# One block for layer norm and feed-forward in a six-layer decoder kernel

## The chip, the core and the metric

The kernel runs on one core of one Trainium2 chip. Its engines each follow an instruction stream of their own: TensorE (PE in the profile, PEld for its weight loads), VectorE (DVE), ScalarE (ACT), GpSimd (POOL) and SyncE (SP, here only a queue that issues DMAs). They meet through semaphores. The metric is the device time of one execution in microseconds (us), lower is better; the number compared is the median of several executions.

## The reference

The program computes a decoder of two layers on x (4 sequences of 256 tokens, 256 columns, so 1024 tokens in 8 tiles of 128). Each layer is self-attention, cross-attention and a feed-forward part, each on a layer norm of x and added to x. The change concerns the feed-forward part of the first layer:

```python
def activation_quant(x, num_bits=8):
    s = qp / jnp.clip(jnp.max(jnp.abs(xf), axis=-1, keepdims=True), EPS, None)   # qp = 127, qn = -128
    return (jnp.clip(jnp.round(xf * s), qn, qp) / s).astype(x.dtype)
...
h = jax.nn.silu(bit_linear(x, w_gate)) * bit_linear(x, w_up)    # 256 -> 1024 columns
h = rms_norm(h, ln_weight)
return bit_linear(h, w_down)                                     # 1024 -> 256
...
x = x + _L0_ffn_ref(_layernorm(x, axis=-1), ...)
```

bit_linear multiplies the quantised activations by weights rounded to -1, 0, 1 times a mean. The second cross-attention, two stages later, uses the input ctx_512 (1024 tokens, 64 columns) as keys and values of 8 groups.

## The kernel before

The program is a sequence of blocks. Inside a block every engine has its own stream; at a block's end all engines and the issued DMAs that the block waits for must be done before the next block starts. The order within a stream is written out by hand. `TT` is 8 token tiles, `c.x` the residual stream, `c.ps` the 8 PSUM banks, `wb` the ternary weights in bf16.

The feed-forward part (`ffn_stages`) is three blocks. First `layer_norm` writes normalised tiles to `c.xn` (L200 to L217). Then comes the gate/up block: VectorE takes the largest magnitude of all eight tiles in one reduction (L1871), makes the factors, and quantises all tiles by multiply and min, max and add of the rounding constant, subtract (L1885 to L1893); TensorE turns all 16 quarter tiles (L1909), ScalarE copies them out (L1940), and then for each tile TensorE makes gate and up products in four PSUM banks (L1919), ScalarE applies silu to the gate half (L1946), VectorE multiplies it by the up half into `h` (L1899), and ScalarE sums squares of `h` (L1933). Silu of tile t stands before the squares of tile t-1. VectorE also splits the alibi slopes into bf16 parts (L1808 to L1822), and GpSimd writes ones into rows of the key stack (L110).

The third block is the down product. Per tile: ScalarE multiplies `h` by the reciprocal root (L1982), GpSimd multiplies it by `ln_weight` (L2006), VectorE finds the largest magnitude (L2026), makes factors (L2029 to L2035), quantises in three passes over 128x1024 (L1763, L1765, L1767), TensorE turns the tile (L2064), ScalarE copies it out (L1991), TensorE multiplies by the down weights (L2055), VectorE adds to x (L2020). The residual add of tile t-1 stands behind the quantising of tile t. Beside it `ContextKeys` makes the keys of the later cross-attention: transposes at the head (L2110), copies and a three-part bf16 split on ScalarE and GpSimd (L2116 to L2136), eight ScalarE instructions that clear `kx` (L2124), and on SP the DMAs that scatter the parts, behind the last of the clears:

```python
        sp.wait_ge(self.zeroed.sem, self.zeroed.at(self.CLEARS))
        for part, done in enumerate((self.hi_done, self.mid_done, self.lo_done)):
```

After it comes the second self-attention (`attention_block`), whose first VectorE instruction is L477.

Of the kernel before, what the change touches and what calls it, by code (L numbers as in the profile page):

```python
# [23 lines left out]
P = 128  # L24
# [6 lines left out]
BANK = 512  # L31
# [1728 lines left out]
def quantise(dve, tile, scale, out, sig, first, n):  # L1760


    dve.tensor_scalar(tile, tile, scale, INT8_MAX, ALU.mult, ALU.min).then_inc(sig.sem, 1)  # L1763
    dve.wait_ge(sig.sem, first + 1)
    dve.tensor_scalar(tile, tile, INT8_MIN, ROUND, ALU.max, ALU.add).then_inc(sig.sem, 1)  # L1765
    dve.wait_ge(sig.sem, first + 2)
    dve.tensor_scalar(out, tile, -ROUND, None, ALU.add).then_inc(sig.sem, 1)  # L1767


class AlibiRows:  # L1770
# [18 lines left out]
    def moves(self, sp):  # L1789
# [13 lines left out]
        sp.wait_ge(self.filled.sem, 16 * 4 * RINGS)  # L1803

    def split(self, dve):
        parts, wide, step = self.parts, self.wide, self.step
        dve.wait_ge(self.loaded.sem, 48)
        dve.tensor_copy(self.c.maskb[:, :, :], self.maskf[:, :, :]).then_inc(step.sem, 1)  # L1808
        dve.tensor_copy(parts[:, 3:6, :], self.pos[:, :].unsqueeze(1).broadcast_to([16, 3, SEQ])).then_inc(step.sem, 1)

        dve.tensor_scalar(self.slope[:, 1:2], self.slope[:, 0:1], 1.0 / self.scale, None, ALU.mult)\
            .then_inc(step.sem, 1)
        dve.wait_ge(step.sem, 3)
        dve.tensor_copy(wide[:, 0, :], self.slope[:, 1:2].broadcast_to([16, SEQ])).then_inc(step.sem, 1)
        for k in range(3):
            dve.wait_ge(step.sem, 4 + 2 * k)
            dve.tensor_copy(parts[:, k, :], wide[:, k, :]).then_inc(step.sem, 1)
            if k < 2:
                dve.wait_ge(step.sem, 5 + 2 * k)
                dve.tensor_tensor(wide[:, k + 1, :], wide[:, k, :], parts[:, k, :], ALU.subtract).then_inc(step.sem, 1)  # L1820
        dve.wait_ge(step.sem, 9)
        dve.tensor_scalar(parts[:, 6:9, :], parts[:, 0:3, :], -1.0, None, ALU.mult).then_inc(step.sem, 1)  # L1822
        dve.wait_ge(step.sem, 10)


def ffn_stages(c, keys):


    nc, io = c.nc, c.io
    with ExitStack() as st:  # L1830
        wb, mean = c.wb, c.fmean
        layer_norm(c, "ln3", want_t=False)

# [1175 lines left out]
```

## Time and profile before

| what | us |
|---|---|
| median of 3 runs (lowest, highest) | 927.35 (925.09, 927.48) |
| the profiled execution, its own time | 919.2 |
| its span, first to last instruction | 917.3 |
| of it the three blocks that change, first instruction to the next block's first | 110.1 |
| TensorE busy over the span | 751.6 |
| VectorE busy over the span | 587.8 |
| ScalarE busy over the span | 439.2 |
| GpSimd busy over the span | 208.3 |

Busy time is the sum of an engine's instructions; where it is short of the span the engine waited. "PEclk" in a row is TensorE's granted clock as a share of 2.4 GHz (0.50 is 1.2 GHz throughout). A bracket at the end of a timeline row is the idle time of that engine before the instruction and what ended it.

### The profile page before, as it was taken

What the parts mean: (1) busy time and instruction counts of PE and PEld (TensorE: products, weight loads), DVE (VectorE), ACT (ScalarE), POOL (GpSimd) and SP (SyncE); (2) the same over time, 40 slices, a digit from 0 to 9 for tenths busy, and PEclk for the clock granted to TensorE, in tenths of its full rate; (3) what the DMA queues carried; (4) which work ended last, traced back from release to release, by engine and by line L of the source; (5) the groups of instructions that cost most, each with busy time, mean ns of one, the idle gap of its engine ahead of it and who ended that gap; (6) DMA issues with size and microseconds to landing.
All of it is one profiled execution on the core that took longest, in us unless ns stands there. A gap on an engine that the chain in (4) does not pass through costs nothing. (4 is left out here: it accounts for less than half of the span.)

```text
span 917.3 us, 13384 instructions
## 1 busy us (share of the span) xinstructions
PE 751.6 (82%) x4838; PEld 480.8 (52%) x4850; DVE 587.8 (64%) x1129; ACT 439.2 (48%) x897; POOL 208.3 (23%) x299
## 2 busy tenths in 40 slices
PE   6999858999899998988363454899939999949998
PEld 3555545666566665665221232556623444438787
DVE  5578475565565655655665974456447999763766
ACT  4568534453634536345255633455344666622332
POOL 2322020311303023030403422322022111242541
PEclk9999989999999999999766556999966999987999
DMA  4533332021111201101120002521010111301211
GB/s 129 150 105 117 103 65 70 29 68 28 43 32 38 68 17 52 27 13 24 42 56 23 1 8 63 145 71 37 2 49 4 46 49 52 104 2 52 88 46 47
DMA packets 48205, 49.65 MB, mean 54 GB/s; under 512 B 9954, under 2 KB 39362, under 8 KB 48138
## 3 DMA queue, kind: packets, MB, share of 16 engines
q1 hardware_dynamic: 44162, 47.77, 18.5%
q10 hardware_dynamic: 3978, 1.02, 0.5%
q8 instruction: 40, 0.66, 0.3%
q14 instruction: 25, 0.20, 0.1%
HBM read 25.69 MB, written 1.16 MB: 29 GB/s over the span
## 5 line engine op out<-in xcount | busy, mean ns | idle before, releaser
L2343 DVE TENSOR_REDUCE x_nm<-ps 128x2 f32<-128x512 f32 x128 | 84.9, 686 | 18.0 <-PE ps L2474 15.7
L522 DVE TENSOR_REDUCE a_nm<-ps 128x2 f32<-128x512 f32 (+1 forms) x112 | 75.3, 688 | 30.9 <-PE ps L824 18.5
L2420 ACT ACTIVATE x_pt<-ps 128x1024 f32<-128x1024 f32 x64 | 62.5, 1021 | 36.3 <-PE ps L2502 36.3
L1446 ACT ACTIVATE m_junk<-ps,m_nm 128x256 bf16<-128x256 f32 x128 | 58.7, 486 | 36.6 <-DVE m_nm L1309 36.6
L1569 PE MATMUL ps<-m_xp,m_mp 128*128 128x512 f32 x288 | 73.6, 396 | 2.0 <-DVE m_wr L1297 2.0
L1283 DVE TENSOR_TENSOR m_qcs<-ps,mw_tab 128x512 f32<-128x512 f32 x96 | 61.8, 686 | 20.5 <-PE ps L1569 19.6
L1269 POOL TENSOR_SCALAR fw<-fw,finv 128x256 f32<-128x256 f32 x24 | 11.6, 484 | 253.4 <-PE ps L1649 253.4
L1569 PEld LDWEIGHTS ps<-m_xp,m_mp 128*128 128x128 f32 x288 | 51.4, 188 | 14.1 <-issue 5.0
L2474 PE MATMUL ps<-kx,a_qs 96*128 96x256 bf16 x256 | 53.4, 296 | 1.9 <-DVE x_nm L2343 1.7
L2835 PE MATMUL ps<-x_xp,x_wp 128*128 128x512 f32 x216 | 54.6, 403 | 0.3 <-DVE x_h3g L2757 0.3
L2835 PEld LDWEIGHTS ps<-x_xp,x_wp 128*128 128x128 f32 x216 | 40.5, 193 | 9.0 <-issue 0.4
L2517 PE MATMUL ps<-x_pt,a_ks 128*32 128x256 f32 x512 | 41.8, 399 | 0.8 <-DVE x_av L2350 0.6
L1309 DVE TENSOR_REDUCE m_nm<-ps 128x2 f32<-128x512 f32 x64 | 39.9, 682 | 3.4 <-PE ps L1608 3.2
L1332 DVE TENSOR_TENSOR m_cp<-ps,m_cp 128x256 fp32r<-128x256 f32 x32 | 12.8, 422 | 43.8 <-ACT m_cp L1472 43.8
L2474 PEld LDWEIGHTS ps<-kx,a_qs 96*128 96x128 bf16 x256 | 20.4, 101 | 37.2 <-issue 13.6
L2502 PE MATMUL ps<-a_qs,kx 98*128 98x512 bf16 x128 | 39.8, 394 | 0.0
L1608 PE MATMUL ps<-m_kHH,m_qs 128*128 128x256 f32 x128 | 35.9, 317 | 4.3 <-DVE m_qs L1302 4.2
L1648 PE MATMUL ps<-m_qs,m_kHH 128*128 128x512 f32 x64 | 27.7, 432 | 13.0 <-issue 8.9
L1466 ACT ACTIVATE m_pt<-ps 128x1024 f32<-128x1024 f32 x32 | 31.1, 1019 | 13.3 <-PE ps L1649 13.3
L667 ACT ACTIVATE a_pt<-ps 128x1024 f32<-128x1024 f32 x32 | 32.1, 1021 | 10.7 <-PE ps L859 10.7
L667 ACT ACTIVATE fw<-ps 128x1024 f32<-128x1024 f32 (+1 forms) x32 | 25.8, 810 | 21.9 <-PE ps L875 15.2
L1339 DVE TENSOR_TENSOR x<-ps,x 128x512 f32<-128x512 f32 x32 | 22.1, 691 | 21.7 <-PE ps L1679 19.8
(292 smaller groups left out, 1769.4 us busy)
## 6 DMA issues: line engine op xcount, KB each, us to landing
a_qs<-a_parts SPq DMA_DIRECT2D x48, 128.0 KB
a_ks<-a_parts SPq DMA_DIRECT2D x48, 128.0 KB
m_q<-m_qs SPq DMA_DIRECT2D x32, 128.0 KB
x_gb<-scr_g SPq DMA_DIRECT2D x8, 512.0 KB, 3.8
fw<-in_f_w SPq DMA_DIRECT2D x12, 256.0 KB
a_qs<-a_ks SPq DMA_DIRECT2D x48, 64.0 KB
mw_wq<-in_m_wq SPq DMA_DIRECT2D x8, 256.0 KB, 2.9
mw_wo<-in_m_wo SPq DMA_DIRECT2D x8, 256.0 KB, 2.9
```

Source lines behind the costliest of these rows:

```text
L522: dve.tensor_reduce(dst, src, AX.X, ALU.max, negate=True).then_inc(mx_done.sem, 1)
L667: act.activation(pt[:, n % 2, kt, 0:banks * BANK], c.ps[:, 2 + 2 * kt:2 + 2 * kt + banks, :].rearrange("p b n -> p (b n)"), ACT.Exp, scale ...
L1283: dve.tensor_tensor(qcs[:, half, tile, cs, :].rearrange("p (b q) -> p b q", q=SEQ), c.ps[:, QB_BANKS[k], :].rearrange("p (b q) -> p b q", ...
L1309: dve.tensor_reduce(nm[:, k // 4, first:first + QT], c.ps[:, S_BANKS[k % 4], :].rearrange("p (t k) -> p t k", t=QT), AX.X, ALU.max, negate ...
L1446: act.activation(junk[:, n % 4, :], c.ps[:, S_BANKS[k % 4], qt * SEQ:(qt + 1) * SEQ], ACT.Exp, bias=nm[:, k // 4, one], accum_out=den[:, k ...
L1569: mm = pe.matmul(c.ps[:, QB_BANKS[k], :], mp[:, p % 2, w, dt, tile * P:(tile + 1) * P], xp[:, x, dt, half_cols(half)], start=((dt, w, x) = ...
L2343: dve.tensor_reduce(nm[:, n % ITEMS, QT * u:QT * u + QT], c.ps[:, u % 2, :].rearrange("p (t k) -> p t k", t=QT), AX.X, ALU.max, negate=Tru ...
L2420: act.activation(pt[:, n % 2, kt, :], c.ps[:, 2 + 2 * kt:4 + 2 * kt, :].rearrange("p b n -> p (b n)"), ACT.Exp, scale=SCALE).then_inc(exp_ ...
L2474: mm = pe.matmul(c.ps[:, u % 2, qt * SEQ:(qt + 1) * SEQ], queries(slice(0, S_ROWS), n, u).squeeze(1)[:, qt * P:(qt + 1) * P], kx[0:S_ROWS, ...
L2502: mm = pe.matmul(c.ps[:, 2 + 2 * kt + h // 2, :], kx[0:T_ROWS, g, b * SEQ + kt * P:b * SEQ + (kt + 1) * P], queries(slice(0, T_ROWS), n, h ...
L2517: mm = pe.matmul(c.ps[rows(h), 6, 0:SEQ], vs[:, QT * b + kt, g, :], pt[:, n % 2, kt, h * SEQ:(h + 1) * SEQ], start=(kt == 0), stop=(kt == ...
L2835: mm = pe.matmul(up_bank(j, half), wp[:, b, w, at:at + EH], xp[:, x, dt, cols(half)], start=((dt, w, x) == terms[0]), stop=((dt, w, x) == ...
```

## The change

The three blocks become one, `feed_forward`.

- The tiles are only centred (x minus mean); the largest magnitude is taken of the centred tile and the root of the variance goes into the factors. Likewise `h` is not multiplied by the reciprocal root: GpSimd multiplies `h` by `ln_weight` as soon as the squares of that tile are summed, and the root goes into the factors once all sums are there.
- Clipping to -128 and 127 is left out of the quantising, since the scaled values cannot pass 127: two VectorE instructions instead of three. In the second quantising ScalarE makes the multiplication for six of the eight tiles.
- Factors are made for groups of tiles (2 and 6, then 6 and 2) and not tile by tile.
- Every tile goes through turning, copy, gate, up by itself, starting with tile 0. In ScalarE's stream the squares of tile t-1 now stand before silu of tile t. Largest magnitudes of `h` are found within this loop, three tiles behind.
- In the second loop TensorE turns tile t+1 before the down product of tile t, and VectorE adds residual t before it rounds tile t+3.
- The keys are transposed and copied at the block's head, cleared by one DMA of zeros and sent by SP as soon as their parts are there. The alibi split moves from VectorE to GpSimd, ahead of GpSimd's part in keys and `h`; the rows of ones come by DMA from a small tile that GpSimd sets.

The diff, cut to the streams (signals, declarations and the text of unchanged helpers are left out):

```diff
@@ class AlibiRows
-    def split(self, dve):
-        dve.wait_ge(self.loaded.sem, 48)
-        dve.tensor_copy(self.c.maskb[:, :, :], self.maskf[:, :, :]).then_inc(step.sem, 1)
...
+    def split(self, pool):
+        pool.wait_ge(self.loaded.sem, 48)
+        pool.tensor_copy(self.c.maskb[:, :, :], self.maskf[:, :, :]).then_inc(step.sem, 1)
+        pool.tensor_copy(parts[:, 3:6, :], self.pos[:, :].unsqueeze(1).broadcast_to([16, 3, SEQ])).then_inc(step.sem, 1)
...
@@ def feed_forward
+    EARLY = 2
+    GROUPS = (slice(0, EARLY), slice(EARLY, TT))
+    GROUPS2 = (slice(0, 6), slice(6, TT))
+    ON_VECTOR = (1, 4)
...
+            @block.sync
+            def _(sp):
+                keys.load(sp)
+                alibi.loads(sp)
+                sp.dma_start(lnw, io["f_ln"].broadcast_to([P, FFN])).then_inc(lnw_in.sem, 16)
...
+                keys.clear(sp)
+                alibi.moves(sp, keys)
+                keys.send(sp)
...
+            @block.gpsimd
+            def _(pool):
+                keys.constants(pool)
+                alibi.split(pool)
+                keys.remainder(pool)
+                pool.wait_ge(lnw_in.sem, 16)
+                for t in range(TT):
+                    pool.wait_ge(sq_done.sem, sq_done.at(t + 1))
+                    pool.tensor_tensor(h[:, t, :], h[:, t, :], lnw, ALU.mult).then_inc(g_done.sem, 1)
+                    if t == 2:
+                        keys.low(pool)
...
+                def quantised(t):
+                    dve.tensor_scalar(xc[:, t, :], xc[:, t, :], qsc[:, one(t)], ROUND, ALU.mult, ALU.add)\
+                        .then_inc(scaled.sem, 1)
+                    dve.wait_ge(scaled.sem, t + 1)
+                    dve.tensor_scalar(xq[:, t, :], xc[:, t, :], -ROUND, None, ALU.add).then_inc(xq_done.sem, 1)
...
+                for t in range(EARLY):
+                    centred(t)
+                dve.tensor_scalar(mean[:, :], c.fmean[:, :], 1.0 / INT8_MAX, None, ALU.mult).then_inc(mean_done.sem, 1)
+                largest_centred(GROUPS[0])
+                scales(0)
+                for t in range(EARLY):
+                    quantised(t)
+                for t in range(EARLY, TT):
+                    centred(t)
+                largest_centred(GROUPS[1])
+                gated(0)
+                scales(1)
+                quantised(2)
+                quantised(3)
+                gated(1)
+                for t in range(2, TT):
+                    if t + 2 < TT:
+                        quantised(t + 2)
+                    if t > 2:
+                        largest(t - 3)
+                    gated(t)
+                largest(5)
+                dve.wait_ge(sq_done.sem, sq_done.at(TT))
+                dve.tensor_scalar(std2[:, :], ssq[:, :], 1.0 / FFN, RMS_EPS, ALU.mult, ALU.add).then_inc(var2_done.sem, 1)
+                scales2(0)
+                rounded(0)
+                rounded(1)
+                largest(6)
+                largest(7)
+                scales2(1)
+                rounded(2)
+                for t in range(TT):
+                    residual(t)
+                    if t + 3 < TT:
+                        rounded(t + 3)
...
+                keys.order(act)
+                act.wait_ge(var_done.sem, var_done.at(1))
+                act.activation(std[:, :], std[:, :], ACT.Sqrt).then_inc(std_done.sem, 1)
+                act.preload_act_table_set("silu_and_others")
+                copied(0)
+                copied(1)
+                keys.copies(act)
+                silu(0)
+                silu(1)
+                square(0)
+                keys.middle(act)
+                for t in range(2, TT):
+                    copied(t)
+                    square(t - 1)
+                    silu(t)
+                act.preload_act_table_set("sqrt_and_others")
+                square(TT - 1)
...
+                turn(0)
+                turn(1)
+                keys.turn(pe)
                 for t in range(TT):
...
+                    gate(t)
+                    up(t)
+                    if 1 <= t < TT - 1:
+                        turn(t + 1)
+                turn2(0)
                 for t in range(TT):
...
+                    if t + 1 < TT:
+                        turn2(t + 1)
+                    down(t)
@@ class ContextKeys
-        sp.wait_ge(self.zeroed.sem, self.zeroed.at(self.CLEARS))
         for part, done in enumerate((self.hi_done, self.mid_done, self.lo_done)):
```

ScalarE's stream in the gate/up loop of the kernel before, from its first silu (L1946 is silu, L1933 the squares, x2 two in a row):

```order
L1946 ACT_TABLE_LOAD
L1946 ACTIVATE fw<-ps,f_deq 128x1024 x2
L1933 ACTIVATE f_junk,f_ssq<-f_h 128x1024
L1946 ACTIVATE fw<-ps,f_deq 128x1024
L1933 ACTIVATE f_junk,f_ssq<-f_h 128x1024
```

The same place of the changed kernel, from the copies of turned tiles 0 and 1 (L2045; L2224 and L2225 copy the keys, L2055 is silu, L2062 the squares):

```order
L2045 ACTIVATE xnT<-ps 128x2x128 x2
L2224 ACTIVATE kx_full<-ps 64x1024
L2225 ACTIVATE kx_parts<-ps 64x1024
L2055 ACTIVATE fw<-ps,f_deq 128x1024 x2
L2062 ACTIVATE f_junk,f_ssq<-f_h 128x1024
L2229 ACTIVATE kx_parts<-kx_rest 64x1024
L2045 ACTIVATE xnT<-ps 128x2x128
L2062 ACTIVATE f_junk,f_ssq<-f_h 128x1024
L2055 ACTIVATE fw<-ps,f_deq 128x1024
```

Before, silu of tile t+1 stood between silu and squares of tile t; from tile 2 on now silu of a tile stands behind the squares of the tile before it, and the two copies of the keys stand ahead of the first silu.

GpSimd's stream from its first instruction in these blocks, before:

```order
L110 MEMSET a_ks 32x6144
L1857 UNCONDITIONAL_BRANCH
L2001 UNCONDITIONAL_BRANCH
L2006 TENSOR_TENSOR f_h<-f_h,fw 128x1024 x4
L2131 TENSOR_TENSOR kx_rest<-kx_full,kx_parts 64x1024
```

And of the changed kernel (L1803 to L1817 are the alibi split, L2245 and L2250 the keys, L1907 the multiplication by `ln_weight`):

```order
L1812 CAST al_parts<-al_wide 16x256
L1817 TENSOR_SCALAR al_parts<-al_parts 16x768
L2245 TENSOR_TENSOR kx_rest<-kx_full,kx_parts 64x1024
L1907 TENSOR_TENSOR f_h<-f_h,fw 128x1024 x3
L2250 TENSOR_TENSOR kx_parts<-kx_rest,kx_parts 64x1024
L1907 TENSOR_TENSOR f_h<-f_h,fw 128x1024 x5
```

The multiplications moved from the down block into the gate/up loop, behind the split and the first part of the keys, with the last part of the keys after the third of them.

VectorE's stream around one tile of the second loop, before:

```order
L1763 TENSOR_SCALAR f_h<-f_h,f_qs 128x1024
L1765 TENSOR_SCALAR f_h<-f_h 128x1024
L1767 TENSOR_SCALAR fw<-f_h 128x1024
L2020 SCALAR_TENSOR_TENSOR x<-ps,f_dd,x 128x256
L2026 TENSOR_REDUCE f_am<-f_h 128x1
```

And from the first rounding to the second residual of the changed kernel (L1987 and L1984 round into the bf16 tile, L1981 multiplies, L1957 is the largest magnitude, L1994 the residual add):

```order
L1987 TENSOR_SCALAR fw<-f_h 128x1024
L1981 TENSOR_SCALAR f_h<-f_h,f_qsc 128x1024
L1984 TENSOR_SCALAR fw<-f_h 128x1024
L1957 TENSOR_REDUCE f_big<-f_h 128x1 x2
L1964 SCALAR_TENSOR_TENSOR f_amax<-f_std,f_big 128x2
L1969 RECIPROCAL f_qsc<-f_amax 128x2
L1971 TENSOR_SCALAR f_qsc<-f_qsc 128x2
L1973 SCALAR_TENSOR_TENSOR f_deq<-f_amax,f_mean,f_inv 128x2
L1987 TENSOR_SCALAR fw<-f_h 128x1024
L1994 SCALAR_TENSOR_TENSOR x<-ps,f_deq,x 128x256
```

Of a tile's work in this loop one rounding and one residual add are left, and residual 0 now stands behind the rounding of tile 2 and ahead of that of tile 3.

## Rows read from the trace of the kernel before

**Rows 1.** Timeline, edges of the stages: start us, us, engine, line, operation.

```profile
446.74 1.28 ACT L234 ACT_TABLE_LOAD   x1 [4.48 <-PEq L1219]
...
471.74 1.11 ACT L1946 ACTIVATE fw<-ps,f_deq 128x1024 f32<-128x1024 f32 x1 [2.39 <-PE ps L1919]
...
488.66 1.28 DVE L1899 SCALAR_TENSOR_TENSOR f_h<-ps,f_deq,fw 128x1024 f32<-128x1024 f32 x1 [1.10 <-ACT fw L1946]
...
503.93 0.13 PEld L2064 LDWEIGHTS ps<-identb,fw 128*128 128x128 bf16 x2 [11.06 <-DVE fw L1767]
...
548.84 0.48 DVE L2020 SCALAR_TENSOR_TENSOR x<-ps,f_dd,x 128x256 f32<-128x256 f32 x1 [3.74 <-PE ps L2055]
...
552.37 0.68 SPq L2146 DMA_DIRECT2D kx<-a_ks  x1
...
556.88 0.43 DVE L477 BATCH_NORM_STATS2 a_stats<-x 128x6 f32<-128x256 f32 x1 [7.56 <-PEq L1969]
```

**Rows 2.** Busy time by stretch: both loops; then PEclk, DMA share.

```profile
468.00:491.20 23.20, 17.05 (x62) 6.30 (x64) 11.22 (x11) 18.32 (x26) 0.00 (x0) 0.87 0.12 16
...
503.90:546.90 43.00, 21.41 (x120) 13.47 (x120) 39.80 (x63) 22.68 (x24) 16.95 (x7) 0.50 0.00 0
```

**Rows 3.** Groups in 446.7 to 556.9: count, busy us, mean ns, idle before.

```profile
L2006 POOL TENSOR_TENSOR f_h<-f_h,fw 128x1024 f32<-128x1024 f32 x8 | 19.2, 2413 | 55.6 <-DMA fw<-in_f_ln 36.1 <-ACT f_h L1982 19.5
...
L2055 PE MATMUL ps<-wb,fw 128*128 128x256 bf16 x64 | 15.1, 418 | 9.7 <-ACT fw L1991 9.7
...
L1765 DVE TENSOR_SCALAR f_h<-f_h 128x1024 f32<-128x1024 f32 x8 | 13.5, 1683 | 0.3
...
L1899 DVE SCALAR_TENSOR_TENSOR f_h<-ps,f_deq,fw 128x1024 f32<-128x1024 f32 x8 | 10.3, 1283 | 10.7 <-ACT fw L1946 10.7
...
L2026 DVE TENSOR_REDUCE f_am<-f_h 128x1 f32<-128x1024 f32 x8 | 9.7, 1210 | 4.5 <-POOL f_h L2006 4.5
...
L1946 ACT ACTIVATE fw<-ps,f_deq 128x1024 f32<-128x1024 f32 x8 | 8.9, 1110 | 4.5 <-PE ps L1919 4.5
...
L1933 ACT ACTIVATE f_junk<-f_h 128x1024 bf16<-128x1024 f32 x8 | 8.4, 1048 | 0.3 <-DVE f_h L1899 0.3
...
L2064 PE MATMUL ps<-identb,fw 128*128 128x128 bf16 x64 | 8.3, 311 | 22.5 <-DVE fw L1767 22.5
...
L1991 ACT ACTIVATE fw<-ps 128x1024 bf16<-128x1024 bf16 x8 | 8.2, 1023 | 27.8 <-PE ps L2064 27.8
...
L2020 DVE SCALAR_TENSOR_TENSOR x<-ps,f_dd,x 128x256 f32<-128x256 f32 x8 | 3.8, 478 | 3.9 <-PE ps L2055 3.9
...
L1885 DVE TENSOR_SCALAR xn<-xn,f_qsc 128x256 f32<-128x256 f32 x8 | 2.2, 348 | 0.0
...
L2110 PE MATMUL ps<-ident,kx_ordered 128*64 128x128 f32 x8 | 1.9, 418 | 4.0 <-PEq L1857 4.0
...
L2035 DVE TENSOR_SCALAR f_qs<-f_qs 128x1 f32<-128x1 f32 x8 | 1.2, 153 | 0.0
...
L2116 ACT ACTIVATE kx_full<-ps 64x1024 f32<-64x1024 f32 x1 | 1.0, 1006 | 0.0
```

**Rows 4.** Timeline, VectorE and GpSimd side by side in the second loop.

```profile
512.84 4.79 DVE L1765 TENSOR_SCALAR f_h<-f_h 128x1024 f32<-128x1024 f32 x1
...
514.75 2.33 POOL L2006 TENSOR_TENSOR f_h<-f_h,fw 128x1024 f32<-128x1024 f32 x1
...
521.28 0.69 DVE L1765 TENSOR_SCALAR f_h<-f_h 128x1024 f32<-128x1024 f32 x1
```

**Rows 5.** Timeline, the reordering of the context at the head.

```profile
457.62 1.13 ACT L2103 ACTIVATE kx_ordered<-kx_raw 128x512 f32<-128x512 f32 x1 [6.93 <-DMA kx_raw<-in_ctx]
```

**Rows 6.** DMA issues: KB each, median us from issue to landing.

```profile
kx_raw<-in_ctx SPq DMA_DIRECT2D x1, 256.0 KB, 3.7
```

**Rows 7.** Groups of GpSimd over the whole span: one input.

```profile
L1273 POOL TENSOR_SCALAR wb<-fw 128x256 bf16<-128x256 f32 x24 | 20.6, 858 | 2.0
...
L2276 POOL COPY a_ks<-kx_raw 128x512 f32<-128x512 f32 x1 | 0.6, 611 | 0.1
```

More of the change, by code:

```diff
@@ L1757 @@
 FT = FFN // P
[L1760 to L1767, printed above, removed]
 class AlibiRows:
@@ L1830, in ffn_stages, with feed_forward @@
+        pool.wait_ge(step.sem, 9)
+        pool.tensor_scalar(parts[:, 6:9, :], parts[:, 0:3, :], -1.0, None, ALU.mult).then_inc(step.sem, 1)
+        pool.wait_ge(step.sem, 10)
+def feed_forward(c, keys):
+    nc, io = c.nc, c.io
+    EARLY = 2
+    GROUPS = (slice(0, EARLY), slice(EARLY, TT))
+    GROUPS2 = (slice(0, 6), slice(6, TT))
+    ON_VECTOR = (1, 4)
+    ON_SCALAR = tuple(t for t in range(TT) if t not in ON_VECTOR)
     with ExitStack() as st:
-        wb, mean = c.wb, c.fmean
-        layer_norm(c, "ln3", want_t=False)
@@ L1887, in _ @@
-                for g in range(HALF):
-                    some = slice(g * TT // 2, (g + 1) * TT // 2)
-                    dve.wait_ge(q_s.sem, 2 * g + TT)
-                    dve.tensor_scalar(c.xn[:, some, :], c.xn[:, some, :], INT8_MIN, ROUND, ALU.max, ALU.add)\
-                        .then_inc(q_s.sem, 1)
-                    dve.wait_ge(q_s.sem, 2 * g + TT + 1)
-                    dve.tensor_scalar(xq[:, some, :], c.xn[:, some, :], -ROUND, None, ALU.add).then_inc(q_s.sem, 1)
-                alibi.split(dve)
@@ new lines, in down @@
+                def down(t):
+                    pe.wait_ge(hqT_done.sem, hqT_done.at(t + 1))
+                    if t >= 2:
+                        pe.wait_ge(x_done.sem, x_done.at(t - 1))
+                    for f in range(FT):
+                        mm = pe.matmul(c.ps[:, 2 + t % 2, 0:DIM], hqT[:, t % 2, f, :], wb[:, 2, f * DIM:(f + 1) * DIM],
+                                       start=(f == 0), stop=(f == FT - 1))
+                    mm.then_inc(y_done.sem, 1)
+                turn(0)
@@ L2069 @@
+        for s in (var_done, std_done):
+            s.done(1)
 class ContextKeys:
     GROUPS, S_ROWS, T_ROWS, HD = 8, 96, 98, 8
-    CLEARS = 8
     def __init__(self, c, st):
@@ L2900, in build_program @@
             keys = ContextKeys(c, st)
-            ffn_stages(c, keys)
+            feed_forward(c, keys)
             w = c.a1_w
```

409 lines of the change are left out of this document (212 added, 197 removed).

## The prediction

> **What bounds the kernel now.** I read the timeline between the last instruction of the first cross-attention and the first of the second self-attention, since only that stretch changes. Its edges [rows 1] give five pieces: head, from 446.74 to the first silu at 471.74, 25.0 us; gate/up loop, to the end of the last product at 489.94, 18.2 us; turnaround, to the first turned quarter of `h` at 503.93, 14.0 us; second loop, to the end of the last residual add at 549.32, 45.4 us; tail, to VectorE's next instruction at 556.88, 7.6 us, while the keys' DMAs, the last issued at 552.37, land. In all 110.1 us.
>
> Each piece has its own limit. In the gate/up loop TensorE is busy for 17.05 of 23.2 us and ScalarE for 18.3, at a granted clock of 0.87; a tile takes 2.2 us. In the second loop VectorE is busy for 39.8 of 43.0 us and TensorE for half, at a granted clock of 0.50, that is 1.2 GHz throughout [rows 2]. But VectorE's busy time there holds waiting: L1765 is the same operation eight times, 1.68 us in the mean [rows 3], yet 0.69 when GpSimd is idle and 4.79 when it starts beside a GpSimd instruction and another follows at once [rows 4]. So an fp32 tensor_scalar from SBUF to SBUF stands still while GpSimd works. Reductions (1.21 us) and products that read PSUM (L1899, 1.28 in the mean) show no such spread.
>
> The Trainium skill, page "SBUF — State Buffer", section "Who interferes with whom", says that VectorE in a two-port mode and GpSimd exclude each other for a whole instruction, whoever starts first. Read as it stands it makes the new gate/up loop, where GpSimd is busy 2.4 of 3.5 us, a place where a late tensor_scalar costs up to one multiplication; that is the stall I price below from the rows.
>
> **The change, piece by piece.** I write the new streams out from the block's start at 446.7 with the durations of before.
>
> *Head.* The context lands 3.7 us after its issue [rows 6], is reordered in 1.13 [rows 5], then the root's table loads in 1.28 [rows 1] and the root takes 0.2: VectorE, which is done with statistics and centring at about 452, gets the roots at 453.2. Small factor operations are 0.15 each in the mean [rows 3], near 0.2 with their waits: five or six, 1.2 us. One 128x256 tensor_scalar is 2.2/8 = 0.27 us [rows 3], about 0.35 with its wait, two per tile. GpSimd is now in the alibi split, so I add one short GpSimd instruction, 0.3 to 0.5, to most of them: tile 0 quantised at 455.7, tile 1 at 456.9. TensorE turns tile 1, then the keys (1.9 us), to 459.2; ScalarE copies them twice (1.0 each [rows 3]) ahead of the first silu: 461.2. The head takes 14.5 instead of 25.0: **gain 10.5**.
>
> *GpSimd's split.* The trace has no such cast on GpSimd. A copy of 512 columns takes 0.61, a clipping cast of 256 columns 0.86 [rows 7], so between 1.2 and 3.4 ns a column. The split has some 2,800 single-input columns and two subtractions: 6.4 us by the copy, about 14 by the clip. I take the copy, since it is the same operation but for the output type. From the masks' landing at about 452.6 the split ends at 460, before the keys' copies are there.
> The skill's page "GPSIMD Engine Reference", section "4.1 Engine selection", names VectorE for elementwise work and puts GpSimd near line rate with one input but about 2x slower with two. Doubling VectorE's 4.0 us of split gives 8 us, an estimate, and the end at 461; nothing then waits longer, so the sum would stay.
>
> *Gate/up loop.* Silu 1.1, product 1.28, squares 1.05 [rows 3]. Before, silu of t+1 ran beside the product of t. Now the order in ScalarE's stream is squares t-1, silu t, and the squares wait for the product t-1, which waits for silu t-1. The three stand in a ring: 1.1 + 1.28 + 1.05 = 3.43, with hand-overs **3.45 us a tile instead of 2.2**. TensorE needs at the higher clock about 2.2 of it, at 1.2 GHz about 4 (eight 128x512 products are twice L2055's 1.89 per tile), so it keeps up once the clock is up. VectorE has 2.1 us for two tensor_scalars and one reduction (0.6 + 1.2). GpSimd's multiplication of t-1 (2.41) starts when silu t does and ends with product t, so the next quantising just passes it. Two places don't pass: quantising tiles 2 and 3 around the first multiplication (+2.3), and tile 6, when the keys' low part follows at once (+2.3). Written out: first silu 461.2, first product ends at 464.0 (gate and up at 1.2 GHz), the second at 469.8 (factors 1.0, four tensor_scalars 1.2, stall 2.3, product 1.28), six periods 20.7, stall 2.3: last product ends at 492.8. This is 31.6 instead of 18.2: **loss 13.4**.
>
> *Turnaround.* Before it had a block end, a table load, the root, a multiplication on ScalarE, one on GpSimd, reduction, factors and three passes. Now: squares 1.1, variance 0.2 (it starts together with GpSimd's last multiplication, both released by the same squares; I take it as stalled, +2.4, it could be 0), root 0.2, five small operations 0.9, one ScalarE pass about 1.1, one rounding 0.7: 499.5, that is 6.7 instead of 14.0: **gain 7.3**.
>
> *Second loop.* GpSimd is silent here. Tile 1 needs a multiply and a round (1.4), then two reductions (2.4), factors (0.8) and the rounding of tile 2 (0.7): 504.8. From there TensorE has six turns and seven down products. At 1.2 GHz they are 1.03 and 1.89 (8.3 and 15.1 over eight [rows 3]): 3.05 a tile with hand-overs, no gap, end at 524.9. But TensorE is then busy without a break, and in the gate/up loop such a stretch got 0.87 [rows 2]. 0.87 over 23.2 us is six us at 0.50 and the rest at full clock, and about the first four of the six were busy ones. I let it rise after four such us, at 509; then ScalarE's copy (1.02) and multiplication and TensorE's 1.6 share the limit at 1.6 to 2.2 a tile, and the last residual add ends at 518.8. So 19.3 instead of 45.4: **gain 26.1**. About 13 us of it were stalls and third passes on VectorE, the rest the chain of the tile that nothing overlapped.
>
> *Tail.* The keys' low part is made after the third multiplication, at about 479.5; SP then has one part to send, some 40 us before the block's end. SP's wait for the alibi rows ahead of it (split at 460, fourteen issues) is over by 475. A block boundary costs 0.4, so **gain 7.2**. If that cover were gone it costs the 7.6 again.
>
> Sum: 10.5 - 13.4 + 7.3 + 26.1 + 7.2 = 37.7 us. The profiled execution's own 919.2 becomes 881.5; it was 8.2 below the median of the runs shown, 927.35, and the same saving from the median gives **889.7**. Nothing behind the block changes: TensorE idles more than 4 us before the next block in both, and starts it at 1.2 GHz in both.
>
> **The rivals.**
> A. *Fewer stalls.* VectorE's small and short operations slip between GpSimd's, as L2035 seems to have done (0.15 in the mean [rows 3], with half of the eight beside GpSimd's multiplications). Without any stall the same writing-out ends at 511.2: saving 45.2, time 882.1. Against it: the 4.79. Chance 0.22.
> B. *TensorE stays at 1.2 GHz in the second loop.* Saving 37.7 - 6.1 = 31.6, time 895.8. For it: 0.50 over 43 us before; against it, busy share then was half, now nearly all. Chance 0.17.
> C. *The split at the price of the clip.* Eight us more GpSimd work inside the head: first silu at 467, quantising stalled throughout, end at 526.9: saving 29.6, time 897.8; with B 905.8. Chance 0.10.
> D. *Slower than before.* One mechanism: the next block, which reaches the higher clock after its first 7 us and then is busy nearly throughout, stays at 1.2 GHz. Its products would take twice as long; from some 43 us of such a stretch on (busy share near 0.87) the 37.7 are eaten, and at 60 us the time is 942. Nothing in the profile speaks for it. Chance 0.01. That the gate/up loop's ring alone undoes the change needs 5 us a tile more, which no row offers.
> The forecast has 0.50.
>
> **How the numbers follow.** The likeliest case gives 889.7. A reaches down to 882, B and C up to 898; the range 881 to 899 leaves out B with C, D and a little of each end, less than 2 in 10. All cases but D are faster by over 0.3%; I take 0.02 from them for what I have not seen. Those 0.3% are about what a measurement of this kernel can tell from no change.
>
> **What the changed profile would show.** The first silu 14 to 15 us after the block's start; silu to silu 3.4 to 3.5 us, with ScalarE's squares idle before them until VectorE's product; single tensor_scalars of 128x256 of over 2 us beside GpSimd's multiplication or the keys; the variance at 0.2 or 2.5 us; TensorE's clock above 0.50 in the second loop and turns plus products at 1.6 us a tile late in it; the next block 0.4 us behind the last residual add. Wrong if the split's cast shows over 3 us, if VectorE loses a whole multiplication in every tile (+2.4 a tile, 14 us), or if SP still holds the block's end.

## The result, and the profile after

| | before | after |
|---|---|---|
| median (lowest to highest), 4 runs each | 927.41 (925.09 to 928.57) | 882.27 (879.94 to 885.51) |
| ratio, 95% interval | | 0.9555 (0.9518 to 0.9592) |
| profiled execution, its own time | 919.2 | 885.51 |
| its span | 917.3 | 883.5 |

The changed kernel is faster by 4.4%. The ratio of 0.9555 is 41 us, the medians are 45.1 apart, and the block itself is 41.2 us shorter. The edges of its pieces, in the timeline of the kernel after, answer to [rows 1]; L1998 is the block's first instruction, L2055 the first silu, L1952 the last product, L2144 the first turned quarter, L1994 the last residual add, L477 the next block:

```profile
453.93 2.71 DVE L1998 BATCH_NORM_STATS2 f_stats<-x 128x6 f32<-128x256 f32 x8 [0.54 <-PEq L1219]
...
467.16 1.10 ACT L2055 ACTIVATE fw<-ps,f_deq 128x1024 f32<-128x1024 f32 x1
...
498.90 1.28 DVE L1952 SCALAR_TENSOR_TENSOR f_h<-ps,f_deq,fw 128x1024 f32<-128x1024 f32 x1 [1.29 <-ACT fw L2055]
...
506.20 1.03 PE L2144 MATMUL ps<-identb,fw 128*128 128x128 bf16 x8 [7.69 <-DVE fw L1987]
...
521.85 0.48 DVE L1994 SCALAR_TENSOR_TENSOR x<-ps,f_deq,x 128x256 f32<-128x256 f32 x1 [0.74 <-PE ps L2153]
...
522.86 0.43 DVE L477 BATCH_NORM_STATS2 a_stats<-x 128x6 f32<-128x256 f32 x1 [0.53 <-PEq L1884]
```

| piece, us | before | forecast | after |
|---|---|---|---|
| head | 25.0 | 14.5 | 13.2 |
| gate/up loop | 18.2 | 31.6 | 33.0 |
| turnaround | 14.0 | 6.7 | 6.0 |
| second loop | 45.4 | 19.3 | 16.1 |
| tail | 7.6 | 0.4 | 0.5 |
| together | 110.1 | 72.4 | 68.9 |

Busy time of both loops in the kernel after, columns as in [rows 2]:

```profile
467.20:500.20 33.00, 18.69 (x70) 7.08 (x69) 26.73 (x33) 20.34 (x31) 20.90 (x9) 0.84 0.19 41
506.20:522.40 16.20, 13.29 (x128) 10.49 (x128) 12.21 (x23) 12.15 (x13) 0.00 (x0) 0.85 0.01 1
```

The gate/up loop has no engine that fills it any more: TensorE works 18.7 of 33.0 us, ScalarE 20.3, and VectorE's 26.7 hold the time in which it stood still. In the second loop GpSimd is silent, VectorE works 12.2 us instead of 39.8, and the granted clock is 0.85 instead of 0.50.

The two profiled executions also differ where the kernels are the same: the block starts at 446.74 before and at 453.93 after. The stretch from 20 to 60 us, far ahead of the block, shows it, first in the kernel before, then in the one after:

```profile
20.00:60.00 40.00, 36.27 (x211) 21.45 (x209) 24.71 (x40) 22.77 (x41) 12.91 (x22) 1.00 0.42 115
```

```profile
20.00:60.00 40.00, 36.55 (x155) 20.18 (x154) 20.05 (x32) 19.32 (x36) 10.74 (x16) 0.84 0.36 99
```

TensorE was granted 1.00 in one and 0.84 in the other. In the eleven other profiles below the block starts anywhere from 446.61 to 452.29. So all sizes are read from the block's own stretch, and the rest is taken out: 41.2 less 7.2 is 34.0, and the own times of the two profiled executions differ by 33.7. Behind the block both kernels take the same, 360.4 and 360.6 us from L477 to the end of the span.

The ring in the gate/up loop, in the timeline of the kernel after:

```profile
475.92 1.09 ACT L2055 ACTIVATE fw<-ps,f_deq 128x1024 f32<-128x1024 f32 x1
...
477.15 1.28 DVE L1952 SCALAR_TENSOR_TENSOR f_h<-ps,f_deq,fw 128x1024 f32<-128x1024 f32 x1 [1.73 <-ACT fw L2055]
...
478.47 1.06 ACT L2062 ACTIVATE f_junk<-f_h 128x1024 bf16<-128x1024 f32 x1 [1.18 <-DVE f_h L1952]
...
479.52 1.09 ACT L2055 ACTIVATE fw<-ps,f_deq 128x1024 f32<-128x1024 f32 x1
```

Each waits for the one ahead: silu, the product, the squares, the next silu, 3.60 us a tile. The 3.45 of the forecast was the sum of the three with almost nothing for the hand-overs. Twice a quantising pass stood still beside GpSimd; the dearer place, in the same timeline:

```profile
482.01 2.27 POOL L2250 TENSOR_TENSOR kx_parts<-kx_rest,kx_parts 64x1024 bf16<-64x1024 f32 x1
...
482.33 4.40 DVE L1945 TENSOR_SCALAR xnT<-xn 128x256 bf16<-128x256 f32 x1
...
484.25 2.33 POOL L1907 TENSOR_TENSOR f_h<-f_h,fw 128x1024 f32<-128x1024 f32 x1
```

An operation of 0.29 us stands through the keys' low part and through the multiplication behind it, as L1765 did in [rows 4]. From that tile's product to the next are 7.04 us, 3.4 more than a period. What is late after it is the turning of that tile and so TensorE. The other was at 471.32, 2.32 us. The turnaround of the kernel after:

```profile
501.40 0.17 DVE L2027 TENSOR_SCALAR f_std<-f_ssq 128x8 f32<-128x8 f32 x1
501.44 2.34 POOL L1907 TENSOR_TENSOR f_h<-f_h,fw 128x1024 f32<-128x1024 f32 x1 [1.34 <-ACT f_junk L2062]
501.61 0.21 ACT L2093 ACTIVATE f_std<-f_std 128x8 f32<-128x8 f32 x1 [0.24 <-DVE f_std L2027]
501.92 1.88 DVE L1964 SCALAR_TENSOR_TENSOR f_amax<-f_std,f_big 128x6 f32<-128x6 f32 x1 [0.35 <-ACT f_std L2093]
```

The variance started 0.04 us before GpSimd's last multiplication and got through in 0.17. The next operation, two inputs of 6 columns from SBUF, then waited nearly as long: 1.88 us.

### The profile page after: what moved, and what is told of

Read it like the earlier page. It is cut to its first block and busy times, and to the rows that moved or that the text cites. A ratio compares the mean times of both kernels' runs of the same rounds, so it can differ in the third digit from the quotient of the medians.

```text
span 883.5 us, 13351 instructions
## 1 busy us (share of the span) xinstructions
PE 753.8 (85%) x4838; PEld 483.1 (55%) x4850; DVE 565.4 (64%) x1091; ACT 430.7 (49%) x892; POOL 210.9 (24%) x310
## 5 line engine op out<-in xcount | busy, mean ns | idle before, releaser
L2456 DVE TENSOR_REDUCE x_nm<-ps 128x2 f32<-128x512 f32 x128 | 84.9, 686 | 18.1 <-PE ps L2587 15.7
L1332 DVE TENSOR_TENSOR m_cp<-ps,m_cp 128x256 fp32r<-128x256 f32 x32 | 12.8, 422 | 43.8 <-ACT m_cp L1472 43.8
L2587 PEld LDWEIGHTS ps<-kx,a_qs 96*128 96x128 bf16 x256 | 20.4, 101 | 37.2 <-issue 13.6
```

The costliest lines, as they stand in the source:

```text
L2456: dve.tensor_reduce(nm[:, n % ITEMS, QT * u:QT * u + QT], c.ps[:, u % 2, :].rearrange("p (t k) -> p t k", t=QT), AX.X, ALU.max, negate=Tru ...
L2587: mm = pe.matmul(c.ps[:, u % 2, qt * SEQ:(qt + 1) * SEQ], queries(slice(0, S_ROWS), n, u).squeeze(1)[:, qt * P:(qt + 1) * P], kx[0:S_ROWS, ...
```

## The experiments

Each is the changed kernel with the edit shown, unless another is named, profiled once and timed. They were compared with the kernel before in three groups, whose medians of before were 924.91 (the first four), 923.63 (the next four) and 921.04 (the last three). Pieces are head, gate/up loop, turnaround, second loop, tail; the changed kernel has 13.2, 33.0, 6.0, 16.1, 0.5, together 68.9.

The pieces are read from one profile each, and the same code does not take the same time in all of them: the gate/up loop of the changed kernel took 33.0, 33.0, 33.3 and 34.3 us (after, e10, e7, e8), and e5 and e6, whose edits differ only in the turnaround, 27.2 and 25.4 there and 17.2 and 16.1 in the second loop. By the timed ratios only e9 (faster) and e10 (slower) have intervals that lie clear of the changed kernel's 0.9518 to 0.9592; e7's just meets it, and the others overlap it. What the text says of a piece rests on the timelines.

**e1_silu_first: the ring.**

```diff
                     copied(t)
-                    square(t - 1)
                     silu(t)
+                    square(t - 1)
```

> In ScalarE's stream of the gate/up loop silu of tile t stands ahead of the squares of tile t-1 again. The changed kernel's three blocks' stretch, from the block's first instruction to the next block's first, is 68.9 us; a tile takes 3.6 us. Theory 1 (the ring of silu, product and squares sets the tile): the tile falls to about 3.2 us, where VectorE's own 3.1 us of work takes over, and the stretch shortens by 1.5 to 2.5 us. Theory 2 (GpSimd's multiplications set it through VectorE's tensor_scalars that stand still beside them): VectorE now meets GpSimd in the middle of a multiplication, the stalls grow by what the ring gives, and the stretch stays within 0.5 us or grows.

882.24 us, ratio 0.955 (0.952 to 0.9581), stretch 65.9: 13.1, 28.2, 6.9, 17.2, 0.5. The loop gives 4.8 us and the stretch 3.0, more than the 1.5 to 2.5 of theory 1; the ratio shows nothing of it (0.955 against 0.9555). The 4.8 are not the ring alone: three stalls of over 2 us stand in the loop (466.66, 471.88, 477.53), but the one of 4.40 is gone. The cleaner comparison is e3 with e2, below. Of the 2.0 us that come back, 1.1 are in the second loop, where this profile shows TensorE's higher clock only 9.3 us into it and the changed kernel's 4.8.

**e2_low_last: the keys' low part behind the last multiplication.**

```diff
-                    if t == 2:
+                    if t == TT - 1:
```

> GpSimd's last part of the keys stands behind the eighth multiplication and not behind the third. Theory 1 (the 4.40 us tensor_scalar of tile 6 is on the chain, and TensorE's 4.5 us of idling behind it puts the next tile at 1.2 GHz): the stretch of 68.9 us shortens by 3.5 to 4.5 us, no tensor_scalar of 128x256 over 3 us is left, and the keys' last DMA, issued about 7 us before the block's end, is still hidden. Theory 2 (a wait put off, the next multiplication takes its place): the stretch shortens by less than 1 us. Theory 3 (the tail comes back): SP holds the block's end by 2 us or more and the gain is gone.

880.47 us, ratio 0.9522 (0.9493 to 0.9551), stretch 66.8: 13.2, 29.2, 7.7, 16.1, 0.5. The loop gives 3.8 us: the 4.40 stall cost nearly all of itself. But the turnaround grows by 1.7, since a factor operation of 0.17 now stands beside the low part, and the stretch gains only 2.1, less than theory 1's 3.5 to 4.5. The timeline of this kernel:

```profile
494.20 1.88 DVE L1964 SCALAR_TENSOR_TENSOR f_amax<-f_std,f_big 128x6 f32<-128x6 f32 x1 [0.35 <-ACT f_std L2093]
...
496.02 2.11 POOL L2250 TENSOR_TENSOR kx_parts<-kx_rest,kx_parts 64x1024 bf16<-64x1024 f32 x1
...
496.34 1.82 DVE L1971 TENSOR_SCALAR f_qsc<-f_qsc 128x6 f32<-128x6 f32 x1
```

The tail stays 0.5, though SP sends the last keys only at 498.8.

**e3_ahead_low_last: both, with the copy of the next tile ahead of the squares.**

```diff
+                copied(2)
                 for t in range(2, TT):
-                    copied(t)
-                    square(t - 1)
                     silu(t)
+                    if t + 1 < TT:
+                        copied(t + 1)
+                    square(t - 1)
...
-                    if t == 2:
+                    if t == TT - 1:
```

> Both edits, and the copy of the next turned tile between silu and squares, so that TensorE gets it early. Theory 1 (ring and the keys' part add up): the stretch of 68.9 us shortens by 5 to 7 us, a tile takes 2.9 to 3.2 us. Theory 2 (VectorE and GpSimd exclude each other whatever the order): no more than what moving the keys' part alone gives, a tile stays at 3.4 to 3.7 us.

876.49 us, ratio 0.9487 (0.9455 to 0.952), stretch 62.8: 12.8, 25.4, 7.8, 16.1, 0.5. The loop gives 7.6 us and the stretch 6.1, as theory 1 had it. Against e2, which has the keys' part in the same place, the new order alone gives 3.8 us of the loop: that is what the ring cost. Now VectorE sets the loop, with its stalls: it is busy for 24.8 of 25.4 us, and its work for a tile in the middle, without a gap, is 3.2.

**e4_split_vector: the alibi split back on VectorE, ahead of the first product.**

```diff
-                alibi.split(pool)
...
                 largest_centred(GROUPS[1])
+                alibi.split(dve)
                 gated(0)
```

> The alibi split back on VectorE, between the second reduction of centred tiles and the first product. Theory 1 (VectorE's own time decides: 4.0 us of split against about 2 us of stalls that GpSimd's split causes at the head): the first product starts 2 us later and the stretch of 68.9 us grows by 1.5 to 2.5 us. Theory 2 (the stalls cost as much as the split): the stretch stays within 0.7 us.

884.4 us, ratio 0.9573 (0.9524 to 0.9623), stretch 71.1: 11.7, 36.7, 6.0, 16.1, 0.5. The head is 1.5 shorter, with no cast beside the centring passes; the first product ends 17.8 us after the start instead of 15.7. On balance the stretch is 2.2 us longer, within theory 1's 1.5 to 2.5, so by the profiles the move to GpSimd is worth that much; the timed ratios are too close to show it.

**e5_low_after_fifth: e3 with `if t == 4` for the low part.**

> As the run with the copy ahead and the keys' part last (stretch 62.8 us, turnaround 7.8), but the keys' last part stands behind the fifth multiplication, where VectorE has no tensor_scalar left until the variance. Theory 1 (what made the turnaround 1.8 us longer was the small tensor_scalar of the factors standing still for 1.82 us beside the keys' part): the turnaround is 6.0 to 6.4 us and the stretch 60.8 to 61.6 us. Theory 2 (GpSimd's backlog moves to the last multiplication and holds VectorE there instead): the turnaround stays over 7 us.

874.85 us, ratio 0.9497 (0.9441 to 0.9554), stretch 65.7: 13.4, 27.2, 7.4, 17.2, 0.5. Theory 1 failed and theory 2 came: GpSimd's backlog reaches the variance, which stood 3.14 us at 488.51. The stall moves, it does not go. Against e3 the stretch is 2.9 us longer: 1.8 in the gate/up loop, where two quantising passes now stand one behind the other (2.06 at 469.36, 2.32 at 471.46), and 1.1 in the second loop, where the higher clock came 9.7 us into the loop instead of 3.4. The ratio does not tell e5 from e3.

**e6_factors_psum: e5 with roots and reciprocals in PSUM.**

```diff
-        ssq, std2, inv2 = sb("ssq", [P, TT]), sb("std2", [P, TT]), sb("inv2", [P, TT])
+        ssq, var2, inv2 = sb("ssq", [P, TT]), sb("var2", [P, TT]), sb("inv2", [P, TT])
+        std2, rec2 = c.ps[:, 4, 0:TT], c.ps[:, 5, 0:TT]
```

> As the run before it, and the roots of the second factors and their reciprocals are written to PSUM, so that the operations that make the first group's factors have at most one input in SBUF. Theory 1 (VectorE stands still beside GpSimd where both inputs are in SBUF, or input and output of a tensor_scalar): the 1.88 us operation on the factors falls to 0.2, the turnaround shortens by 1.5 to 1.8 us and so does the stretch. Theory 2 (any VectorE operation of two inputs, or the wait has another cause): it stays at 1.9 us.

876.63 us, ratio 0.9518 (0.9445 to 0.959), stretch 63.3: 13.6, 25.4, 7.6, 16.1, 0.5. The timeline of this kernel, VectorE alone:

```profile
492.66 3.37 DVE L2028 TENSOR_SCALAR f_var<-f_ssq 128x8 f32<-128x8 f32 x1
496.35 0.17 DVE L1965 SCALAR_TENSOR_TENSOR f_amax<-ps,f_big 128x6 f32<-128x6 f32 x1 [0.32 <-ACT ps L2096]
```

The turnaround of 7.6 is not the shorter one of theory 1. In e5 and e6 the variance reads SBUF alone and stands, 3.14 and 3.37. The factor operation, with one input from PSUM, takes 0.17, but GpSimd was done at 496.00 (and in e5, from SBUF alone, it took 0.17 too once GpSimd was done), so e6 by itself does not show that PSUM frees it.

**e7_turn_behind_down: no overlap of tiles in the second loop.**

```diff
+                    down(t)
                     if t + 1 < TT:
                         turn2(t + 1)
-                    down(t)
```

> The changed kernel with TensorE's turn of tile t+1 behind the down product of tile t. Its second loop is 16.1 us. If what carries the loop is the overlap of tiles: a tile becomes turn, copy and product in a row, 0.62 + 1.02 + 1.04 us at 2.4 GHz with hand-overs of 0.3, 3.0 us a tile, and the loop takes 22 to 23 us; if TensorE's gaps (a busy share near 0.55) also bring the clock down to 1.2 GHz, 4.2 us a tile and 31 to 32 us. If VectorE and ScalarE bound the loop anyway: under 18 us.

888.47 us, ratio 0.9655 (0.9592 to 0.9717), stretch 76.3: 13.2, 33.3, 6.0, 23.2, 0.5. The overlap is worth 7.1 us. The clock did not stay at 1.2 GHz: it rose 4.9 us into the loop, as it did in the changed kernel (4.8). Windows of this kernel's second loop, its first 3.5 us and the rest:

```profile
502.40:505.90 3.50, 2.32 (x15) 1.69 (x16) 3.47 (x5) 2.38 (x3) 0.00 (x0) 0.50 0.02 5
505.90:525.70 19.80, 11.47 (x115) 9.16 (x113) 9.13 (x20) 10.28 (x10) 0.00 (x0) 0.96 0.00 0
```

TensorE worked 11.5 of 19.8 us at 0.96. Before, it worked 21.4 of 43.0 at 0.50 [rows 2].

**e8_gpsimd_busy: eight more multiplications on GpSimd in the second loop, of data that nothing uses.**

```diff
+                pool.wait_ge(h_done.sem, h_done.at(TT))
+                for k in range(TT):
+                    pool.tensor_tensor(c.fw[:, 0, 0:FFN], lnw, lnw, ALU.mult).then_inc(busy.sem, 1)
```

> The changed kernel with eight more multiplications of 128x1024 on GpSimd behind the last one, of data that nobody uses, so that GpSimd is busy for 19 us of the second loop. If VectorE's tensor_scalars stand still beside GpSimd, as the forecast had it for a third of the gain of the second loop: seven or eight of its ten tensor_scalars take up to 2.4 us more, the loop grows from 16.1 to 25 to 28 us. If GpSimd's silence is worth little there: under 19 us, the block's end then being that of GpSimd's extra work.

889.6 us, ratio 0.9653 (0.958 to 0.9726), stretch 79.2: 12.8, 34.3, 8.0, 23.6, 0.5. The timeline of this kernel:

```profile
501.91 4.52 POOL L1915 TENSOR_TENSOR fw<-fw 128x1024 f32<-128x1024 f32 x2
502.30 2.38 DVE L1987 TENSOR_SCALAR f_h<-f_h,f_qsc 128x1024 f32<-128x1024 f32 x1
...
504.71 2.27 DVE L1990 TENSOR_SCALAR fw<-f_h 128x1024 bf16<-128x1024 f32 x1
```

Passes of 0.74 and 0.69 take 2.38 and 2.27. Not all of them do: one at 512.74 slips through at 0.68. The second loop loses 7.5 us and the turnaround 2.0, less than the 9 to 12 forecast for the loop: the eight began at 497.97, in the turnaround, and were over at 515.17, 12.7 us into the loop. The turn of tile 2 begins 11.0 us into the loop instead of 5.0, so 6.1 of the 7.5 lie ahead of it, where VectorE stood. The rest lies behind it, where the clock was still the lower one, up to 16.5 us into the loop. Windows of this kernel's second loop:

```profile
502.44:518.60 16.16, 8.90 (x57) 6.70 (x58) 14.98 (x14) 7.67 (x8) 12.34 (x6) 0.50 0.00 1
...
518.80:526.03 7.23, 6.47 (x72) 5.31 (x70) 4.70 (x9) 4.46 (x5) 0.00 (x0) 0.99 0.00 0
```

**e9_root_scalar: e6 with variance and root in one ScalarE operation, and the low part behind the first multiplication.**

```diff
-                dve.tensor_scalar(var2[:, :], ssq[:, :], 1.0 / FFN, RMS_EPS, ALU.mult, ALU.add).then_inc(var2_done.sem, 1)
...
-                act.activation(std2, var2[:, :], ACT.Sqrt).then_inc(std2_done.sem, 1)
+                act.activation(std2, ssq[:, :], ACT.Sqrt, scale=1.0 / FFN, bias=var2[:, 0:1]).then_inc(std2_done.sem, 1)
```

> Silu ahead of the squares and the copy ahead, factors through PSUM, and now the variance of h and its root in one ScalarE operation, and the keys' last part behind the first multiplication, where GpSimd was idle for 2.6 us. Theory 1 (the turnaround of 7.6 us holds a variance that stands still for up to 3.4 us beside GpSimd, and nothing else to spare): squares 1.1, root 0.2, factors 0.7, multiplication 1.1, rounding 0.7 with hand-overs give 4.2 to 4.8 us, the loop stays at 25.4 to 27, and the stretch is 59 to 61 us. Theory 2 (GpSimd's last multiplication, which ends when it ends, holds the first rounding instead): turnaround 5.2 to 6 us, stretch 61 to 62.

875.1 us (871.07 to 878.81), ratio 0.948 (0.9446 to 0.9514), stretch 61.1: 13.2, 25.6, 4.4, 17.3, 0.5. The timeline of this kernel:

```profile
487.06 4.81 POOL L1909 TENSOR_TENSOR f_h<-f_h,fw 128x1024 f32<-128x1024 f32 x2
...
489.48 0.27 ACT L2096 ACTIVATE ps<-f_ssq,f_var 128x8 f32<-128x8 f32 x1
489.86 0.17 DVE L1966 SCALAR_TENSOR_TENSOR f_amax<-ps,f_big 128x6 f32<-128x6 f32 x1 [0.61 <-ACT ps L2096]
...
490.37 1.52 DVE L1975 SCALAR_TENSOR_TENSOR f_deq<-f_amax,f_mean,f_inv 128x6 f32<-128x6 f32 x1
```

GpSimd is busy from 487.06 to 491.87, and the root on ScalarE and the factor operation with its PSUM input pass beside it in 0.27 and 0.17, where the changed kernel's L1964 took 1.88. The same kernel has the counter-example: L1975, whose inputs all lie in SBUF, stood 1.52 us beside the same GpSimd instruction, until GpSimd was done. No later step waited for it. The turnaround falls from 6.0 to 4.4, as theory 1 had it. This is the lowest of the ratios, but e3's 0.9487 and e5's 0.9497 are not distinct from it; against the changed kernel it is 0.948/0.9555 = 0.992, a quotient that was not measured side by side.

The Trainium skill, page "SBUF — State Buffer", section "Who interferes with whom", gives VectorE and GpSimd one port pair of SBUF that only one of them can hold; by that rule an operation with at most one SBUF input goes free if it is in no two-port mode, and one with two SBUF inputs does not. The trace agrees, with 0.17 and 1.52.

**e10_keys_sent_last: SP's sends of the keys wait for the last residual add.**

```diff
+        sp.wait_ge(self.c.counter("no_x").sem, self.c.counter("no_x").at(TT))
```

> The changed kernel, but SP sends the key parts only when the last residual add is done, as late as the kernel before did. If the tail of 7.6 us was these transfers and nothing else: 0.5 becomes 7 to 9 us (seven issues at 0.65 and a landing) and the stretch grows from 68.9 to 76 to 78 us. If the block's end cost it: no change.

888.87 us, ratio 0.9663 (0.9616 to 0.971), stretch 77.5: 13.4, 33.0, 6.0, 16.1, 9.0. The timeline of this kernel:

```profile
514.85 0.48 DVE L1994 SCALAR_TENSOR_TENSOR x<-ps,f_deq,x 128x256 f32<-128x256 f32 x1 [0.74 <-PE ps L2153]
515.41 4.02 SPq L2258 DMA_DIRECT2D kx<-kx_parts  x6
519.47 0.70 SPq L2259 DMA_DIRECT2D kx<-kx_ones  x1
...
524.31 1.08 DVE L477 BATCH_NORM_STATS2 a_stats<-x 128x6 f32<-128x256 f32 x3 [8.97 <-PEq L1884]
```

Exposed, the sends and their landing cost 8.5 us, and no other piece moves by more than 0.2. That is the cover that the tail's gain rests on.

**e11_clip_back: the clips as a pass of their own, in both quantisings.**

```diff
-                    dve.tensor_scalar(xc[:, t, :], xc[:, t, :], qsc[:, one(t)], ROUND, ALU.mult, ALU.add)\
+                    dve.tensor_scalar(xc[:, t, :], xc[:, t, :], qsc[:, one(t)], INT8_MAX, ALU.mult, ALU.min)\
...
+                    dve.tensor_scalar(xc[:, t, :], xc[:, t, :], INT8_MIN, ROUND, ALU.max, ALU.add)\
```

> The changed kernel with a clip pass of its own back in both quantisings. If VectorE's passes bound the second loop in the kernel before as much as I took them to: VectorE has 1.9 us a tile there, over the 1.6 us of TensorE, and the loop grows from 16.1 to 18.5 to 20 us; the head grows by 0.5 and the turnaround by 0.7, the gate/up loop by 0 to 4 us with where the stalls fall. If the passes hide: the second loop stays within 1 us.

885.35 us, ratio 0.9596 (0.9566 to 0.9627), stretch 75.2: 14.7, 34.1, 6.7, 19.1, 0.5. The third pass costs 3.0 us in the second loop, as forecast, and 3.3 in the three pieces ahead of it.

## Why the prediction was right

The time, 882.27, lies in the range of 881 to 899 and 7.4 below the forecast of 889.7. Of these 7.4, 3.5 are the block (saving 41.2 instead of 37.7). The other 3.9 are the distance of the medians, 45.1, from the block's 41.2. The interval of the ratio, 37.8 to 44.7 us, holds 41.2, and 45.1 lies just above it. No run assigns the 3.9 to a cause. In the block the pieces were off by 1.3, -1.4, 0.7, 3.2 and -0.1 us, so part of the nearness is luck: the gate/up loop's error took some of the others away.

- **Head** (gain 10.5, measured 11.8): the steps hold. The roots were there 5.6 us after the block's start instead of 6.5, which is most of the difference. GpSimd's split took 7.7 us instead of 6.4, and its end, 0.56 us before the keys' copy was there, cost nothing; so the copy's price was near and rival C (the clip's) did not come. Two slips in the working changed nothing: the split has 3,584 single-input columns, not some 2,800 (6.4 and 14 us lie as far apart as some 3,500 columns would put them), and 452.6 with 6.4 gives 459.0, not 460. C together with B comes to 903.9 by the prediction's own terms, not 905.8; both lie outside the range.
- **Gate/up loop** (loss 13.4, measured 14.8): the ring is the mechanism, as e2 and e3 show with 3.8 us between them. Two terms were mis-sized. A period is 3.60 instead of 3.45 us. The stall at the keys' low part, priced at one multiplication (2.3), went through two GpSimd instructions (4.40), though [rows 4] already had such a case; it cost the loop 3.4, and e2 gets 3.8 back. A quicker start of the second product (7.7 us behind the first silu instead of 8.6) hides part of that.
- **Turnaround** (gain 7.3, measured 8.0): the stall was there, but not at the variance, which slipped in at 0.17, but at the operation behind it, 1.88 instead of the 2.4 priced. e9, which also moves the keys' low part and the copies, takes it away and is 1.6 shorter there.
- **Second loop** (gain 26.1, measured 29.3): this is the term that was off most. The six turns and seven down products behind tile 1's reductions begin 5.0 us into the loop, where I had 5.3. But I gave their first four us to 1.2 GHz and let the clock rise then; it was up already, 4.8 us into the loop. In the timeline of the kernel after, the first of these turns takes 0.62 and the product behind it 1.04, where the loop's first turn took 1.03:

```profile
511.16 0.62 PE L2144 MATMUL ps<-identb,fw 128*128 128x128 bf16 x8 [0.83 <-DVE fw L1987]
...
511.62 1.04 PE L2153 MATMUL ps<-wb,fw 128*128 128x256 bf16 x8
```

  From there to the end of the last residual add are 11.2 us, 1.6 for each of seven products, where the forecast had 14.0. My reason for the clock, "busy without a break", is not what it took: it rose at 511.0, while TensorE waited for VectorE, and e7 has it busy for little more than half of the loop and 0.96. Rival B (1.2 GHz throughout) did not come.

  The clock is the smaller part of the 3.2 us. In e1, e5 and e9, with the same second loop, it rose 9.3 to 9.9 us into the loop, which is where the forecast had it (9.5), and the loops took 17.2 to 17.3. Windows of the second loop up to the rise and behind it, of the kernel after and then of e5:

```profile
506.20:511.00 4.80, 3.77 (x24) 2.66 (x24) 4.66 (x9) 3.99 (x5) 0.00 (x0) 0.50 0.02 3
511.00:522.33 11.33, 9.52 (x104) 7.83 (x104) 7.54 (x15) 8.16 (x9) 0.00 (x0) 1.00 0.00 0
```

```profile
494.56:504.25 9.69, 8.50 (x55) 6.53 (x56) 7.61 (x14) 7.42 (x9) 0.00 (x0) 0.50 0.01 2
504.25:511.77 7.52, 6.76 (x75) 5.46 (x73) 4.70 (x9) 4.95 (x5) 0.00 (x0) 1.00 0.00 0
```

  So 1.1 us are the earlier rise, and the other 2.1 are the price of a tile at the higher clock: the forecast had 1.6 to 2.2 us, 9.8 us behind its rise, and e5 took 7.5.
- **Where the 29.3 are from**: the overlap of tiles 7.1 (e7); GpSimd's silence 7.5 (e8, a later rise of the clock in it, and other GpSimd work than before); the third pass 3.0 (e11). These may overlap each other, and the rest of some 12 us (the root, the reductions and the multiplication that left the tile's chain, and the clock) no run separates. The forecast's "about 13 us of it were stalls and third passes" stands against 7.5 + 3.0.
- **Tail** (gain 7.2, measured 7.0): right, and e10 shows the cover.
- **Rivals**: A, without any stall, forecast a stretch of 64.9; the stalls are there, and the stretch is 68.9. The time near A's 882.1 is chance: 3.5 us of the way to it are the block's, by other terms than A's, and 3.9 are not the block's. D did not come: behind the block nothing changed.

## What to carry to other kernels

When two loops over tiles are fused so that an engine alternates between two tiles, write its order out and look for a ring: "squares of t-1, then silu of t" put three engines' work in series, and another order of the same instructions gave 3.8 us of the loop (e3 against e2). A short VectorE operation beside back-to-back GpSimd work is priced by GpSimd's instructions, not by its own length, and moving the GpSimd work moves the stall to the next such operation (e2, e5); what helped was to give those few operations an operand in PSUM or to ScalarE (e9). A gain in one stage, as the 7.6 us of the tail, rests on cover in another, and one run that takes the cover away measures it (e10, 8.5).

## What was not expected of the hardware

- TensorE held a granted clock of 0.96 for 19.8 us with a busy share of 0.58 (e7), while the kernel before stayed at 0.50 for 43 us with a share of 0.50. What tells the two apart is open.
- The stall cost TensorE speed as well. The 4.40 stall made a product late, so the squares, and so the copy of the next turned tile that stands behind them on ScalarE. TensorE idled 4.49 us for it, and the tile's eight matmuls then took nearly twice what they had: the granted clock was 1.00 up to 490.6, within that idle time, and 0.50 from there to 497.4. In e2, without this stall, it was 1.00 from 476.6 to 493.4. The timeline of the kernel after:

```profile
481.30 1.90 PE L2121 MATMUL ps<-wb,xnT 128*128 128x512 bf16 x8 [0.48 <-ACT xnT L2045]
...
491.57 3.60 PE L2121 MATMUL ps<-wb,xnT 128*128 128x512 bf16 x8 [4.49 <-ACT xnT L2045]
```

- GpSimd's one-input operations are not one price. Its groups over the block, in the kernel after (count, busy us, mean ns):

```profile
L1817 POOL TENSOR_SCALAR al_parts<-al_parts 16x768 bf16<-16x768 bf16 x1 | 2.2, 2164 | 0.1
...
L1803 POOL CAST a_maskb<-fw 128x1024 bf16<-128x1024 f32 x1 | 1.0, 1038 | 3.5 <-DMA fw<-in_masks 3.5
L2233 POOL MEMSET kx_zeros<- 128x1024 bf16 x1 | 1.0, 952 | 0.0
...
L1804 POOL CAST al_parts<-al_pos 16x768 bf16<-16x768 f32 x1 | 0.8, 812 | 0.0
```

  The cast of 1024 columns costs 1.0 ns a column, the bf16 tensor_scalar 2.8. The forecast took the copy's 1.2 for all of them; the one tensor_scalar at 2.16 us instead of 0.9 (768 columns by 1.2) is about the 1.3 us between 6.4 and 7.7.
- Small factor operations are not alike beside GpSimd. Those of one column passed: L2035 of the kernel before took 0.15 in all of its eight cases, four of them beside a multiplication, which is what rival A went by. The changed kernel makes factors for groups of tiles, and tensor_scalars of 2, 6 and 8 columns stood: 1.75 (L1977 in e8, at 510.95), 1.82 (e2) and 3.14 (e5). No run tests what tells them apart.
